# Nine more steps of a graph layer's running maximum get their rows by single-row DMAs from SyncE

## The chip, the cores and the metric

The kernel runs on one core of one Trainium2 chip. The core has TensorE (PE), VectorE (DVE), ScalarE (ACT), GpSimd (POOL) and SyncE (SP), which hands out DMAs; sixteen DMA engines move the data. The metric is the device time of one execution in microseconds; the time before is the median of three runs.

## The reference

```python
# x: [6250, 256]; src, dst: [100000] node numbers, sorted by dst
x_src, x_dst = x[src], x[dst]
theta_x = (x_dst - x_src) @ theta_w.T + theta_b
phi_x = x_src @ phi_w.T + phi_b
e = relu(theta_x + phi_x)
out = segment_max(e, dst, num_segments=x.shape[0])
out = where(isfinite(out), out, 0.0)
y = layernorm(x + out, axis=-1)          # no scale, no shift, eps 1e-5
```

## The kernel before

An edge's message is relu(A[dst] + B[src]) with A = x theta^T + both biases and B = x (phi - theta)^T. As A[dst] is the same for all edges of a node, the kernel takes the maximum of B[src] over the edges of each node and adds A afterwards.

**Tiling.** The 100,000 edges are split over the 128 partitions, 782 to each, in order. A step is one edge of every partition: 128 rows of B of 1 KB each. DVE folds the steps one after the other with one instruction (L720): the new running maximum is max(min(former, reset), row), where `reset` starts a new node. Three steps are a group (GROUP = 3, `START[g]` to `STOP[g]`); there are 261 groups, g = 0 to 260.

**Stages.** First TensorE makes the table B (L523), ACT copies it out of PSUM, SP writes it to HBM as `b_table` (L309); meanwhile POOL fetches 51 steps of rows of x (L385) into `early`. Then comes the main loop over the groups, from about 76 to 970 us. After it, POOL and DVE mend the nodes whose edges cross partitions (fix rows: L404, L413), POOL gathers the maxima by node (L422), and DVE and ACT add A and normalise (L836 to L855, L508), stored by SP (L370, L372).

**Where a step's rows come from.** `row_at(k)` (L694) names the place. 703 steps are gathered by POOL, one indirect DMA of 128 rows each, with the row numbers in `idx` (L397), into one of SLOTS = 18 places of `rows`; ahead of a group POOL waits until the fold that last used the place of the group's last row is done (L395). 51 steps, the first of groups 8, 10, 12 to 108, take x rows fetched early, which TensorE turns and multiplies and ACT copies back into `early` (L539, L547, L456, L460). 28 steps are products of TensorE with one-hot columns (L571, L753) and lie in `far`.

**Order on the engines.** Each engine's queue is written out by hand, and each runs `for g in range(NG)`:

- DVE: three folds, in the first 25 groups the splitting of the table for TensorE (L736, L744), one-hots (L753) and small work. The first two folds write PSUM (`acc`), the third writes `hist`. The third waits until the store of group g - 6 has landed (`s_hout`, HELD = 6), the first until ACT has copied group g - 2.
- ACT: in the first groups the casts of a table pair (L448, L452, which waits for the pair), then the copy of the group's two maxima from PSUM to `hist` (L468), after the folds of the group and the landing of the store of g - 6.
- SP: in groups 1 to 23 the load of table pair g + 1 (L328, into two buffers; it waits until DVE has made the rest of pair g - 1, `s_rest`), seven times a list of sources (L342), then the store of the group's maxima to HBM (L354), which waits for ACT's copy. Twelve times x rows follow (L357, L360), and from group 232 on tiles of x for A (L318).

Groups from LATE = 253 on are folded in `hist` alone.

Small tensors that the change touches: `none` (a row of -FLT_MAX, the former of the first fold, written to HBM at L311), `fix` (set to -FLT_MAX, later filled by L404), `bias2`, `ones` and `diag`, which are read in the preparation before the loop.

Of the kernel before, what the change touches and what calls it, by code (L numbers as in the profile page):

```python
# [5 lines left out]
P = 128  # L6
ALU = mybir.AluOpType
# [6 lines left out]
FLT_MAX = 3.4028234663852886e38  # L14
# [8 lines left out]
AT_ONCE = 4  # L23
HOT = 6
PRODUCT_SPANS = ((27, 61, 6), (61, 95, 6), (95, 123, 6), (123, 151, 6), (151, 179, 6), (179, 205, 6), (205, 231, 5))


def build(nc, x, xt, src, src_t, dst, theta_t, phi_t, theta_b, phi_b, out):
# [31 lines left out]
    for b, (begin, stop, apart) in enumerate(PRODUCT_SPANS):  # L60
        for t in range(NT):
            HOT_AT[begin + 4 + t * (stop - begin - 4) // NT].append((b, t))
        first = stop + 6 if stop % 2 else stop + 7
        BATCH_GROUPS.append([first + apart * j for j in range(AT_ONCE)])
        for j, g in enumerate(BATCH_GROUPS[b]):
            assert START[g] not in EARLY_OF and g < NG and (b + 1 == PRODUCTS or g < PRODUCT_SPANS[b + 1][1] + 2)
            PRODUCT_OF[START[g]] = (b, j)
    SPLIT_BY = PAIRS + 2
    EVACUATE_AT = {stop: b for b, (_, stop, _) in enumerate(PRODUCT_SPANS)}
# [22 lines left out]

    GATHERED = [k for k in range(STEPS) if k not in EARLY_OF and k not in PRODUCT_OF]
    PLACE = {k: i % SLOTS for i, k in enumerate(GATHERED)}
# [16 lines left out]
    with ExitStack() as ctx:  # L111
        def sb(name, shape, dt=F32):
            return ctx.enter_context(nc.sbuf_tensor(name, shape, dt))
# [23 lines left out]
        assert KC * AT_ONCE * P <= 4 * D  # L137
        far = sb("far", [P, AT_ONCE, D])
        sources = sb("sources", [P, AT_ONCE, P], I32)
        short_sources = sb("short_sources", [P, 2, AT_ONCE * P], I16)  # L140
        theta_sb = sb("theta_sb", [P, KC, D])
        diff_sb = sb("diff_sb", [P, KC, D])
        bias = sb("bias", [P, D])
        bias2 = sb("bias2", [P, D])

# [5 lines left out]
        reset = sb("reset", [P, STEPS])  # L151
        none = sb("none", [P, D])
        hi = sb("hi", [P, STEPS], BF16)
# [22 lines left out]
        ident = sb("ident", [P, P])  # L176
        ones = sb("ones", [P, P])
        small = sb("small", [P, 16])
        fix_row = sb("fix_row", [P, 1], I32)
        diag = sb("diag", [P, P])  # L180
        carry_on = sb("carry_on", [P, P])
        scanned = sb("scanned", [P, KC, P + 1])
        fix = sb("fix", [P, D])
        late_max = sb("late_max", [P, D])
        is_fix = sb("is_fix", [P, LATE_STEPS])
# [47 lines left out]
        s_got = [sem(f"rows_gathered{i}") for i in range(LANDED)]  # L233
        s_got_end = sem("last_row_gathered")
        s_fold = sem("steps_folded")
        s_copied = sem("groups_copied")
# [46 lines left out]
        def _(sp):  # L283
# [40 lines left out]
            def load_pair(i):  # L324
# [3 lines left out]
                sp.dma_start(b_pair[:, i % 2, 0:n], pairs[:, 2 * i:2 * i + n]).then_inc(s_pair[i % 2], 16)  # L328

            sp.wait_ge(s_bout[0], 16 * (CHUNKS + 1) // 2)  # L330
            sp.wait_ge(s_bout[1], 16 * (CHUNKS // 2))
            for i in range(2):
                load_pair(i)
            for g in range(NG):
                if 1 <= g < PAIRS - 1:
                    load_pair(g + 1)
                if g in SOURCES_AT:
                    b = SOURCES_AT[g]
                    if b:
                        sp.wait_ge(s_short, b)  # L340
                    k0, apart = START[BATCH_GROUPS[b][0]], START[BATCH_GROUPS[b][1]] - START[BATCH_GROUPS[b][0]]
                    sp.dma_start(sources[:], by_step[:, k0:k0 + (AT_ONCE - 1) * apart + 1:apart, :].broadcast_to(  # L342
                        [P, AT_ONCE, P])).then_inc(s_sources, 16)
                if g == A_FROM - 2:
                    sp.wait_ge(s_hotused, PRODUCTS * NT)
                    for t in range(2 * CHUNK):
                        load_tile(t)
                n, slot = STOP[g] - START[g], g % HELD * GROUP
                if g < LATE:
                    sp.wait_ge(s_copied, g + 1)  # L350
                else:
                    sp.wait_ge(s_fold, STOP[g])
                to = kept_by_p[:, START[g]:STOP[g], :] if g < LATE else late_by_p[:, START[g] - KEPT:STOP[g] - KEPT, :]
                sp.dma_start(to, hist[:, slot:slot + n, :]).then_inc(s_hout[g % HELD], 16)  # L354
                if g == EMPTIED:
                    sp.wait_ge(s_pad, 1)
                    sp.dma_start(x_sb[0:LAST_ROWS, NT - 1, :], x[(NT - 1) * P:N]).then_inc(s_x, 16)  # L357
                if g in X_AT:
                    i = X_AT[g]
                    sp.dma_start(x_sb[:, i * X_TILES:(i + 1) * X_TILES, :], by_load[i]).then_inc(s_x, 16)  # L360
                if g - 1 in A_AT:
                    for t in A_AT[g - 1]:
                        if t + 2 * CHUNK < NT:
                            load_tile(t + 2 * CHUNK)
# [13 lines left out]
        def _(pool):  # L378
# [12 lines left out]
            for g in range(NG):  # L391
# [4 lines left out]
                for k in these:  # L396
# [3 lines left out]
                    ).then_inc(s_got[g % LANDED] if k < STEPS - 1 else s_got_end, 16)  # L400

            for i in range(HELD):
                pool.wait_ge(s_hout[i], 16 * len(range(i, LATE, HELD)))
# [4 lines left out]
            pool.wait_ge(s_ends, 1)  # L408
            pool.wait_ge(s_noneout, 16)
            for i in range(HELD):  # L410
# [18 lines left out]
        def _(act):  # L429
            act.dma_start(dwin, dst).then_inc(s_dst, 16)  # L430
            act.dma_start(bias[:], theta_b.rearrange("(a d) -> a d", a=1).broadcast_to([P, D])).then_inc(s_bias, 16)
            act.dma_start(bias2[:], phi_b.rearrange("(a d) -> a d", a=1).broadcast_to([P, D])).then_inc(s_bias, 16)

# [79 lines left out]
        def _(pe):  # L513
# [14 lines left out]
            pe.wait_ge(s_const, 1)  # L528
            pe.matmul(ps_b[:, 0, 0:P], ones[:], diag[:], start=True, stop=True).then_inc(s_flags, 1)
            pe.wait_ge(s_const, 2)  # L530
# [82 lines left out]
        def _(dve):  # L613
# [26 lines left out]
            nc.vector.memset(edges[:, 0:1], 0.0)  # L640
            nc.vector.memset(ones[:], 1.0)
            nc.vector.memset(fix[:], -FLT_MAX)
            nc.vector.memset(late_max[:], -FLT_MAX)
# [40 lines left out]

            then(nc.vector.tensor_scalar(diag[:], ident[:], small[:, 1:2], None, ALU.mult))
            dve.wait_ge(s_bias, 32)
            nc.vector.tensor_tensor(bias[:], bias[:], bias2[:], ALU.add).then_inc(s_const, 1)
            dve.wait_ge(s_const, 1)
# [5 lines left out]
            def row_at(k):  # L694
                if k in PRODUCT_OF:
                    return far[:, PRODUCT_OF[k][1], :]
                return rows[:, PLACE[k], :] if k in PLACE else early[:, EARLY_OF[k], :]

            former = none[:]
            for g in range(NG):  # L700
                n, slot, at = STOP[g] - START[g], g % HELD * GROUP, g % 2 * 2
                if START[g] in EARLY_OF:
                    dve.wait_ge(s_cbe, EARLY_OF[START[g]] + 1)
                if START[g] in PRODUCT_OF:
                    dve.wait_ge(s_far, 2 * PRODUCT_OF[START[g]][0] + 2)
# [196 lines left out]
```

## Time and profile before

| | |
|---|---|
| median of 3 runs | 1057.68 us (1057.27 to 1057.81) |
| profiled execution: time / span | 1059.1 us / 1057.2 us |
| busy, share of the span | POOL 787.2 us (74%), PE 705.7 (67%), DVE 646.7 (61%), ACT 313.2 (30%) |
| DMA | 250.67 MB, mean 237 GB/s |
| granted TensorE clock, mean | 0.846 |

The span runs from the first to the last instruction of the profiled execution. "SPq" is SP's queue of DMA instructions: its times are those of handing out a DMA, not of moving the data, and the busy shares don't count them. For a DMA of POOL the busy time is that of making its descriptors. "issue" as the cause of idle time means that the engine waited for nothing that the profile shows. A wait is put down to whoever ended it last.

### The profile page before, as it was taken

Reading aid. Unit: us, or ns where it says so; the run is one execution under the profiler, and the core shown is the slowest. Engines: PE = TensorE matmul, PEld = TensorE weight load, DVE = VectorE, ACT = ScalarE, POOL = GpSimd, SP = SyncE. Lnnn points to the kernel's source line nnn. Section 1 sums busy time; section 2 is a strip of 40 time slices with the busy share of each in tenths; the row PEclk is TensorE's granted clock in tenths of the full one; section 3 lists DMA queues with packets and bytes.
Section 4 is the critical chain, followed back from the end, with each engine's and each line's share of the span. In section 5 each row is a group of like instructions: output and inputs, shape, how many; then the busy total and the mean of one; then the engine's idle time right before and its main releaser. Section 6 shows DMA issues by size and latency. Waiting matters only on the chain. (4 is left out here: it accounts for less than half of the span.)

```text
span 1057.2 us, 11054 instructions
## 1 busy us (share of the span) xinstructions
PE 705.7 (67%) x3014; PEld 374.4 (35%) x3067; DVE 646.7 (61%) x1585; ACT 313.2 (30%) x653; POOL 787.2 (74%) x812
## 2 busy tenths in 40 slices
PE   5923345999799979885887687668849866663000
PEld 4821223444455444432333233323313324442000
DVE  5006777665666657664655555555655555667898
ACT  2314565433433342223222221222121111110244
POOL 6777777777777777777777777777777777775773
PEclk9965555999899998998999699979979997986555
DMA  8967888777777777777777777777776678885465
GB/s 248 382 222 244 266 269 275 253 228 232 227 244 227 246 232 241 222 252 228 227 231 249 227 233 245 234 228 232 233 224 222 211 229 296 292 277 173 140 190 156
DMA packets 120631, 250.67 MB, mean 237 GB/s; under 512 B 19205, under 2 KB 61146, under 8 KB 120570
## 3 DMA queue, kind: packets, MB, share of 16 engines
q1 hardware_dynamic: 81498, 143.77, 38.0%
q0 software_dynamic: 38640, 105.53, 35.4%
q10 hardware_dynamic: 432, 0.66, 0.3%
q8 instruction: 24, 0.39, 0.2%
q14 instruction: 37, 0.30, 0.1%
HBM read 134.47 MB, written 115.45 MB: 236 GB/s over the span
## 5 line engine op out<-in xcount | busy, mean ns | idle before, releaser
L397 POOL DMA_INDIRECT rows<-b_table,idx x703 | 682.2, 970 | 214.2 <-issue 186.4
L571 PE MATMUL ps_a<-work,shared 128*128 128x512 bf16 x2008 | 475.2, 389 | 75.2 <-DVE work L753 71.7
L571 PEld LDWEIGHTS ps_a<-work,shared 128*128 128x128 bf16 x2058 | 198.1, 100 | 325.2 <-issue 63.0
L468 ACT COPY hist<-acc 128x512 f32<-128x512 f32 x253 | 148.2, 586 | 548.0 <-DVE hist L720 547.9
L720 DVE SCALAR_TENSOR_TENSOR acc<-hist,reset,rows 128x256 f32<-128x256 f32 x173 | 85.4, 494 | 251.8 <-issue 144.1
L720 DVE SCALAR_TENSOR_TENSOR acc<-acc,reset,rows 128x256 f32<-128x256 f32 x253 | 124.7, 493 | 31.0 <-DMA rows<-b_table,idx 19.1
L720 DVE SCALAR_TENSOR_TENSOR hist<-acc,reset,rows 128x256 f32<-128x256 f32 x253 | 122.3, 483 | 26.6 <-DVE acc L720 0.9
L547 PE MATMUL ps_b<-diff_sb,conv_t 128*128 128x256 f32 x204 | 69.8, 476 | 68.4 <-ACT conv_t L460 68.4
L753 DVE TENSOR_SCALAR work<-short_sources,node 128x512 bf16<-128x512 int16 x343 | 114.4, 373 | 0.3 <-PE ps_a L571 0.2
L595 PE MATMUL ps_a<-theta_sb,shared 128*128 128x256 f32 x196 | 57.0, 447 | 37.6 <-DVE shared L791 29.8
L547 PEld LDWEIGHTS ps_b<-diff_sb,conv_t 128*128 128x128 f32 x204 | 45.4, 234 | 83.1 <-ACT conv_t L460 73.9
L422 POOL DMA_INDIRECT rows<-runmax,end_row x49 | 52.1, 1063 | 16.3 <-issue 14.6
L556 PE MATMUL ps_d<-hi,row_of 128*128 128x270 bf16 (+1 forms) x95 | 35.0, 369 | 43.6 <-DVE row_of L762 43.3
L385 POOL DMA_INDIRECT early<-in_x,idx x51 | 49.5, 971 | 18.9 <-issue 15.2
L595 PEld LDWEIGHTS ps_a<-theta_sb,shared 128*128 128x128 f32 x196 | 41.9, 224 | 52.5 <-issue 46.0
L473 ACT ACTIVATE ps_d<-ps_d,node_up 128x782 f32<-128x782 f32 x49 | 43.9, 896 | 0.0
L557 PE MATMUL ps_d<-lo,row_of 128*128 128x512 bf16 x98 | 35.1, 377 | 3.3 <-DVE row_of L762 3.1
L508 ACT ACTIVATE hist<-hist,shift,rstd 128x256 f32<-128x256 f32 x49 | 25.7, 589 | 29.6 <-DVE shift L821 29.6
L556 PEld LDWEIGHTS ps_d<-hi,row_of 128*128 128x128 bf16 x98 | 10.2, 104 | 67.8 <-DVE row_of L762 59.2
L539 PE MATMUL ps_t<-ident,early 128*128 128x128 f32 x102 | 23.3, 317 | 13.1 <-DMA early<-in_x,idx 13.1
L452 ACT CAST shared<-work 128x512 bf16<-128x512 f32 (+1 forms) x25 | 15.2, 609 | 55.6 <-DMA work<-b_table 42.0
L539 PEld LDWEIGHTS ps_t<-ident,early 128*128 128x128 f32 x102 | 17.0, 168 | 23.9 <-issue 16.0
(133 smaller groups left out, 490.1 us busy)
## 6 DMA issues: line engine op xcount, KB each, us to landing
runmax<-hist SPq DMA_DIRECT2D x260, 384.0 KB, 3.1
rows<-b_table,idx POOLq DMA_INDIRECT x703, 3.5
b_table<-rows SPq DMA_DIRECT2D x7, 896.0 KB, 9.1
shared<-in_xt SPq DMA_DIRECT2D x49, 128.0 KB, 4.2
work<-b_table SPq DMA_DIRECT2D x24, 256.0 KB, 3.9
early<-in_x SPq DMA_DIRECT2D x12, 512.0 KB
out<-hist SPq DMA_DIRECT2D x11, 512.0 KB, 3.0
shared<-in_xt SPq DMA_DIRECT2D x7, 512.0 KB, 9.0
```

The source lines that it names most:

```text
L385: pool.indirect_dma_start(out=early[:, e, :], out_offset=None, in_=x, in_offset=bass.IndirectOffsetOnAxis(ap=idx[:, k:k + 1], axis=0)).the ...
L397: pool.indirect_dma_start(out=rows[:, PLACE[k], :], out_offset=None, in_=b_table, in_offset=bass.IndirectOffsetOnAxis(ap=idx[:, k:k + 1], ...
L422: pool.indirect_dma_start(out=rows[:, slot + i, :], out_offset=None, in_=runmax, in_offset=bass.IndirectOffsetOnAxis(ap=end_row[:, t + i:t ...
L468: nc.scalar.copy(hist[:, slot:slot + n - 1, :], acc[:, at:at + n - 1, :]).then_inc(s_copied, 1)
L473: nc.scalar.activation(dst_rows[:, 0:STEPS], dst_rows[:, 0:STEPS], ACT.Sign, bias=node_up[:, t:t + 1], scale=-1.0, accum_out=in_row[:, t:t ...
L539: mm = pe.transpose(ps_t[:, 0, k * P:(k + 1) * P], early[:, e, k * P:(k + 1) * P], ident[:])
L547: mm = pe.matmul(ps_b[:, 0, :], conv_t[:, k, :], diff_sb[:, k, :], start=(k == 0), stop=(k == KC - 1))
L556: pe.matmul(dst_rows[:, at:at + n], row_of[:], hi[:, at:at + n], start=True, stop=False)
L571: mm = pe.matmul(ps_a[k][:].rearrange("p j d -> p (j d)"), split[:, part, t, k * P:(k + 1) * P], hot[:, i % HOT, :], start=(t == 0 and par ...
L595: mm = pe.matmul(ps_a[t % 2][:, 0, :], xt_late[:, t % (2 * CHUNK), k, :], theta_sb[:, k, :], start=(k == 0), stop=(k == KC - 1))
L720: nc.vector.scalar_tensor_tensor(new, former, reset[:, k:k + 1], row_at(k), ALU.min, ALU.max).then_inc(s_fold, 1)
L753: nc.vector.tensor_scalar(hot[:, i % HOT, :], short_sources[:, b % 2, :], node[:, t:t + 1], None, ALU.is_equal).then_inc(s_hot, 1)
```

## The change

Nine steps, the first of nine odd groups (or the next free ones) after group 26, 52, ..., are taken from POOL's list. Their 1,152 rows are fetched by SP: behind the store of each of the groups 0 to 230 it hands out five DMAs (two at the last), each of one row of `b_table` to one partition of `direct`. The row's address comes from a register of SP; before every sixteenth row sixteen registers are loaded from the table of row numbers in HBM. `direct` holds three steps; from the fourth on, SP waits for the fold of three direct steps before. DVE waits for the 128 rows of a direct step before its group. To make room in SBUF, `none` shares `fix`, and `bias2`, `ones` and `diag` lie in `far`; POOL waits for the write of the empty row before it gathers the fix rows.

```diff
--- before.py
+++ after.py
@@ -22,6 +22,10 @@
+DIRECT = 9
+DIRECT_SLOTS = 3
+ROWS_A_GROUP = 5
+LOADED = 16
@@ -65,6 +69,14 @@
+    DIRECT_OF = {}
+    for m in range(DIRECT):
+        g = -(-P * (m + 1) // ROWS_A_GROUP) + 3
+        while START[g] in EARLY_OF or START[g] in PRODUCT_OF:
+            g += 1
+        DIRECT_OF[START[g]] = m
+    DIRECT_STEPS = list(DIRECT_OF)
+    assert len(DIRECT_STEPS) == DIRECT and DIRECT_STEPS[-1] < START[NG - 8] and P % LOADED == 0
@@ -90,7 +102,7 @@
-    GATHERED = [k for k in range(STEPS) if k not in EARLY_OF and k not in PRODUCT_OF]
+    GATHERED = [k for k in range(STEPS) if k not in EARLY_OF and k not in PRODUCT_OF and k not in DIRECT_OF]
@@ -136,12 +148,16 @@
+        direct = sb("direct", [P, DIRECT_SLOTS, D])
...
-        bias2 = sb("bias2", [P, D])
+        bias2 = far[:, 0, :]
+        ones = far[:, 1, 0:P]
+        diag = far[:, 1, P:2 * P]
...
+        none = fix
@@ -232,6 +246,7 @@
+        s_direct = [sem(f"rows_loaded_one_by_one{m}") for m in range(DIRECT)]
@@ -327,6 +342,20 @@
+            held = {}
+
+            def load_row(i):
+                m, p = divmod(i, P)
+                if p == 0 and m >= DIRECT_SLOTS:
+                    sp.wait_ge(s_fold, DIRECT_STEPS[m - DIRECT_SLOTS] + 1)
+                if p % LOADED == 0:
+                    k = DIRECT_STEPS[m]
+                    held["rows"] = nc.values_load_multi_w_load_instructions(
+                        src_t[k:k + 1, p:p + LOADED], engines=[mybir.EngineType.SP], min_val=0, max_val=N - 1,
+                        skip_runtime_bounds_check_because="src holds row numbers of x")[1]
+                sp.dma_start(direct[p:p + 1, m % DIRECT_SLOTS, :],
+                             b_table[bass.ds(held["rows"][p % LOADED], 1), :]).then_inc(s_direct[m], 16)
+
@@ -352,6 +381,8 @@
                 sp.dma_start(to, hist[:, slot:slot + n, :]).then_inc(s_hout[g % HELD], 16)
+                for i in range(ROWS_A_GROUP * g, min(ROWS_A_GROUP * (g + 1), DIRECT * P)):
+                    load_row(i)
                 if g == EMPTIED:
@@ -399,6 +430,7 @@
+            pool.wait_ge(s_noneout, 16)
             for i in range(HELD):
                 pool.wait_ge(s_hout[i], 16 * len(range(i, LATE, HELD)))
...
-            pool.wait_ge(s_noneout, 16)
@@ -638,8 +669,7 @@
-            nc.vector.memset(fix[:], -FLT_MAX)
@@ -694,6 +724,8 @@
+                if k in DIRECT_OF:
+                    return direct[:, DIRECT_OF[k] % DIRECT_SLOTS, :]
@@ -701,6 +733,8 @@
+                if START[g] in DIRECT_OF:
+                    dve.wait_ge(s_direct[DIRECT_OF[START[g]]], 16 * P)
```

## Rows read from the trace of the kernel before

**Rows 1.** Waits of POOL: who waited for whom, us in total, times, longest.
```profile
POOL rows L397 <- issue: 186.4, 612, 0.3
POOL rows L397 <- DVE hist L720: 14.3, 47, 0.3
POOL rows L397 <- DVE acc L720: 13.4, 44, 0.3
```

**Rows 2.** Line 397 (gathers): duration ns min/median/max, first and last start us.
```profile
L397 POOL DMA_INDIRECT rows<-b_table,idx x703: 942/946/1425, 70.6 to 965.7; - x176
```

**Rows 3.** The chain that ended last, around the last gather: start us, us, what.
```profile
961.77 1.12 POOL rows L397
962.89 0.30 issue
963.20 3.00 DMA rows<-b_table,idx
```

**Rows 4.** Waits of SP's queue, whole span.
```profile
SPq L354 <- ACT hist L468: 694.6, 245, 13.7
SPq L328 <- DVE work L744: 52.0, 23, 4.1
```

**Rows 5.** Line 397 by stretch: window us, length, busy us (x started), clock, DMA, GB/s.
```profile
70.00:110.00 40.00, 30.26 (x30) 0.50 0.67 208
110.00:170.00 60.00, 46.59 (x45) 0.53 0.89 277
```

**Rows 6.** Line 720 (folds) by the same stretches.
```profile
70.00:110.00 40.00, 13.21 (x27) 0.50 0.67 208
110.00:170.00 60.00, 22.66 (x47) 0.53 0.89 277
```

**Rows 7.** Waits in the stretch from 110 to 170 us, one row.
```profile
ACT shared L452 <- DMA work<-b_table: 28.5, 16, 3.3
```

**Rows 8.** Timeline of SP's queue, 110 to 170 us: start us, us, operation, count.
```profile
113.14 0.33 SPq L354 DMA_DIRECT2D runmax<-hist  x1
114.99 0.36 SPq L328 DMA_DIRECT2D work<-b_table  x1
...
166.53 0.33 SPq L354 DMA_DIRECT2D runmax<-hist  x1
169.27 0.33 SPq L328 DMA_DIRECT2D work<-b_table  x1
```

**Rows 9.** Timeline of SP's queue later (merged pieces last from first start to last end).
```profile
170.96 88.30 SPq L354 DMA_DIRECT2D runmax<-hist  x32
...
262.81 100.43 SPq L354 DMA_DIRECT2D runmax<-hist  x34
...
866.96 0.32 SPq L354 DMA_DIRECT2D runmax<-hist  x1
867.33 6.71 SPq L318 DMA_DIRECT2D shared<-in_xt  x14
```

**Rows 10.** Line 354 (store of maxima): duration ns min/median/max.
```profile
L354 SPq DMA_DIRECT2D runmax<-hist x261: 319/320/477, 78.2 to 970.4; - x131
```

**Rows 11.** Lines 370 (106 rows stored) and 311 (one row stored), the same.
```profile
L370 SPq DMA_DIRECT2D out<-hist x1: 264/264/264, 987.9 to 987.9; - x1
...
L311 SPq DMA_DIRECT2D runmax<-none x1: 471/471/471, 59.1 to 59.1; - x1
```

**Rows 12.** Line 372 (output stores of SP): time to landing.
```profile
DMA to landing us min/median/max: 1.7/3.0/3.2
```

**Rows 13.** DMA view: SP's queue (packets, MB, share), then two of its issues.
```profile
q1 hardware_dynamic: 81498, 143.77, 38.0%
...
runmax<-hist SPq DMA_DIRECT2D x260, 384.0 KB, 3.1
...
runmax<-none SPq DMA_DIRECT2D x1, 1.0 KB
```

**Rows 14.** All engines by stretch; last three numbers: clock, DMA share, GB/s.
```profile
260.00:430.00 170.00, 150.68 (x692) 80.68 (x705) 110.29 (x277) 62.70 (x140) 129.48 (x134) 0.94 0.73 236
```

More of the change, by code:

```diff
@@ L143, in build @@
         bias = sb("bias", [P, D])
-        bias2 = sb("bias2", [P, D])
+        bias2 = far[:, 0, :]
+        ones = far[:, 1, 0:P]
+        diag = far[:, 1, P:2 * P]
+        assert D == 2 * P
         early = sb("early", [P, max(EARLY, NT), D])
@@ L151, in build @@
         reset = sb("reset", [P, STEPS])
-        none = sb("none", [P, D])
         hi = sb("hi", [P, STEPS], BF16)
@@ L176, in build @@
         ident = sb("ident", [P, P])
-        ones = sb("ones", [P, P])
         small = sb("small", [P, 16])
         fix_row = sb("fix_row", [P, 1], I32)
-        diag = sb("diag", [P, P])
         carry_on = sb("carry_on", [P, P])
@@ L431, in _ @@
             act.dma_start(bias[:], theta_b.rearrange("(a d) -> a d", a=1).broadcast_to([P, D])).then_inc(s_bias, 16)
-            act.dma_start(bias2[:], phi_b.rearrange("(a d) -> a d", a=1).broadcast_to([P, D])).then_inc(s_bias, 16)
+            act.dma_start(bias2, phi_b.rearrange("(a d) -> a d", a=1).broadcast_to([P, D])).then_inc(s_bias, 16)
             for t in range(NT):
@@ L528, in _ @@
             pe.wait_ge(s_const, 1)
-            pe.matmul(ps_b[:, 0, 0:P], ones[:], diag[:], start=True, stop=True).then_inc(s_flags, 1)
+            pe.matmul(ps_b[:, 0, 0:P], ones, diag, start=True, stop=True).then_inc(s_flags, 1)
             pe.wait_ge(s_const, 2)
@@ L640, in _ @@
             nc.vector.memset(edges[:, 0:1], 0.0)
-            nc.vector.memset(ones[:], 1.0)
-            nc.vector.memset(fix[:], -FLT_MAX)
+            nc.vector.memset(ones, 1.0)
             nc.vector.memset(late_max[:], -FLT_MAX)
@@ L683, in _ @@
             nc.vector.tensor_copy(lo[:], pos.bitcast(I32))
-            then(nc.vector.tensor_scalar(diag[:], ident[:], small[:, 1:2], None, ALU.mult))
+            then(nc.vector.tensor_scalar(diag, ident[:], small[:, 1:2], None, ALU.mult))
             dve.wait_ge(s_bias, 32)
-            nc.vector.tensor_tensor(bias[:], bias[:], bias2[:], ALU.add).then_inc(s_const, 1)
+            nc.vector.tensor_tensor(bias[:], bias[:], bias2, ALU.add).then_inc(s_const, 1)
             dve.wait_ge(s_const, 1)
```

## The prediction

> **What bounds the kernel now.** I read the shares of the engines on the page first: no engine is full, POOL is the fullest, so the question is what its idle time is made of. The view of POOL's waits answers it: nearly all the idle time before the gathers of L397 is "issue", 0.30 us at a time, and the 91 idle times put down to DVE are no longer than 0.3 us each either [rows 1]. So POOL never waits; 0.30 us is the gap that each gather has. The view of line 397 gives 703 gathers between 70.6 and 965.7 us [rows 2], that is 895.1 / 702 = 1.275 us a gather (0.946 median duration, 0.30 gap, and some longer ones). The end of the chain shows that this is what sets the end: gathers back to back, the landing of the last, then the last steps [rows 3]. Behind the last fold some 87 us follow (fix rows, maxima by node, normalisation) that the change leaves alone. The bound is thus the number of gathers on POOL, as long as three others keep up: DVE's folds, ACT's copies, and SP, which stores each group's maxima and has so far mostly waited: 694.6 us for ACT's copies at L354, 52.0 us at L328 [rows 4].
>
> How much room is there? POOL may run 18 gathers ahead of the folds (SLOTS). Up to 170 us the windows count 30 + 45 = 75 gathers [rows 5] and 27 + 47 = 74 folds [rows 6]; nine of those folds (groups 8, 10 to 24) took a row of `early`, so 65 used a gather: POOL is 10 ahead. It needs the last row of a group free, so 18 - 10 - 3 = 5 gathers are left, 6.4 us. The reason for that lead is the loop of table pairs in the first 25 groups: SP loads a pair (L328) when DVE has freed the buffer, ACT waits for it (28.5 us in the stretch from 110 to 170 us) [rows 7], and ACT's copy of the group follows. This stretch runs at 3.8 us a group, slower than POOL; afterwards the folds catch up, 32 stores in 88.3 us (2.76 us each) and then 34 in 100.4 us (2.95 us) [rows 9].
>
> **The change part by part.**
>
> Nine gathers leave POOL: 9 x 1.275 = **11.5 us off**, all on the path, since POOL does not wait [rows 1, 2]. What is late next if POOL is faster is what the rest of this part is about.
>
> SP gets, in each of the groups 0 to 230, five DMAs of one row after the store, 1,152 in all, and before every sixteenth a load of sixteen registers from HBM, 72 in all. What a row costs on SP: a store of 128 rows takes 0.320 us when SP has waited [rows 10]; the one store of 106 rows takes 0.264 us, and the only one-row DMA of the trace 0.471 us, right behind another DMA [rows 11]. The fourteen DMAs at 867 us stand 6.71 / 14 = 0.48 us apart [rows 9]. So the ends are 0.26 + 0.03 (the gap between two issues) = 0.29 us and 0.47 + 0.04 = 0.51 us a row. I take 0.35: small DMAs seem cheaper than full ones, and the first behind the store pays the longer time; the register in the address adds something that no row shows. Five are **1.75 us** (1.45 to 2.55).
>
> The register load is not in the trace. Its lower end is another instruction that SP hands out without waiting, 0.3 us; its upper end, if the sixteen values come in one trip, is the round trip of a short transfer, 1.7 to 2.0 us with 1.7 the shortest landing on SP's queue [rows 12]. I take 1.7, since the load must wait for its data: 1.7 x 5/16 = **0.53 us** a group (0.1 to 0.6). If each value had a trip of its own, even at 0.32 us, it would be 5.1 us a load and 1.6 us a group. The Trainium skill ("Runtime: NRT & Kernel Launch", section "Instruction fetch mechanics") puts a bulk register load at about 200 ns a register, 3.2 us for sixteen; no row here shows it. By it the group would cost SP 0.47 us more, the pair loop would suffer most, and the time would come out near 1060 us, no gain.
>
> With the store and its gap (0.37 us) SP's work is then 0.37 + 1.75 + 0.53 = **2.65 us a group**. Its other DMAs in this stretch (23 pairs, 7 lists of sources, 11 loads of x) add some 18 us in all. SP can be at the store of group 231 no sooner than 78.2 + 18 + 231 x 2.65 = 708 us, against 867.0 us now [rows 9] and 855.5 us wanted. The break-even is (855.5 - 96) / 231 = 3.29 us a group over the whole, 2.76 to 2.95 in the quick groups 24 to 90, where six groups of `hist` and the 18 slots lend some time. At 2.65 this is hidden, with little to spare.
>
> Not hidden is the **pair loop**. What SP is moved past counts: behind the five rows and the register load the next L328 is queued, for it ACT waits, and behind ACT the copy of the group and DVE. From the start of a store to the next L328 there are 1.85 us at 113.1 and 2.74 us at 166.5 [rows 8]; the fifteen such gaps between have a mean of 2.2. With the change they are 0.37 + 1.75 = 2.1 us, and 3.8 us in a group with a register load, about one in three. The mean delay is 0.3 x 1.6 + 0.1 = 0.6 us for each pair; as the loop goes over two groups it costs 0.3 us a group, 5 us over groups 8 to 24, nothing before, where the gaps are 2.7 to 4.4 us. The landings of the pairs get longer by the extra packets; I allow 0.4 us for each of 8 turns, 3 us. Against these 8 us stand at best the 6.4 us of slots from above; but SP's rows also slow the catching-up after 170 us, so I count 3 of them: **5 us back** on POOL's path (0 with cheap rows, 12 with rows at 0.51 us and no cover).
>
> The other edits have one answer. `none` shares `fix`, `bias2`, `ones` and `diag` lie in `far`, one memset goes: all of it is before 76 us, where DVE waits, or has long been read when `far` (group 63) and `fix` (after the last steps) are written; if that cover were gone it would be one memset, under 0.5 us. POOL's wait for the empty row moves ahead of the fix gather; that row was written at 59 us. DVE waits for nine direct steps, each three or more groups (8 us) after its last row was issued, against a landing of 3.1 us for a store [rows 13]. SP's own wait for a slot of `direct` names a fold some 50 groups back. The bytes are the same as before.
>
> **The sum.** 1059.1 us is the profiled execution's own time (span 1057.2). 1059.1 - 11.5 + 5 + 0.5 (waits) = 1053.1 us. The median of the runs shown, 1057.68, lies 1.4 below the profiled one, so for timed runs I predict **1051.7 us**.
>
> **Rivals.**
>
> *SP becomes the bound* (slower). One mechanism: rows cost their upper end, 0.51 us, because every DMA keeps its issuer busy for about as long as the full ones at 867 us [rows 9, 11]. SP then needs 0.37 + 2.55 + 0.53 = 3.45 us a group, and reaches group 231 at 96 + 231 x 3.45 = 893 us, 26 us later than now: 1083.7 us. ACT's copies wait for the stores (`maxima_written`), DVE for both, POOL for the folds. It decides from 3.29 us a group, rows at 0.48 us; sixteen separate trips would do it as well, and by more. For it: the only one-row DMA took 0.471 us. Against it: that DMA had the last full chunk of the table before it, and the 106-row store was short.
>
> *The pair loop takes it all* (no change): rows at 0.40 us with the register load at 2.0 us or more, or no cover in the slots; 11.5 us go into 5 + 6 us of delay in the first 25 groups, 1057.7 us, give or take 2. For it: ACT already waits 28.5 us there [rows 7].
>
> *One DMA engine fills up* (slower). Of the packets on SP's queue, 81,498, the issues of the DMA view account for 81,496 if every DMA of 128 rows is its data packets and 16 more (a store 128 + 16, and so on for the 18 kinds listed from the store to the one-row write), which leaves two for the one-row write of 1 KB [rows 13]: one with data and one for the semaphore, so a row isn't spread over the engines. If all rows go to the same engine, it gets ten packets a group. Its share is 0.73 now [rows 14]; the mean packet of that queue takes 0.38 x 16 x 1057.2 / 81,498 = 0.079 us, which makes 0.79 us of 3.0 and a share of 0.99 in the quick groups, 0.95 later. At 0.104 us a packet it would need 0.73 x 3.0 + 1.04 = 3.23 us a group there, 0.23 too much for 85 groups: +20 - 11.5 = 8 us slower, 1066 us. It decides from 0.081 us a packet. Against it: the share counts waiting too, and the load of one engine moves landings, not POOL's pace, while slots are left. The Trainium skill ("DMA: Bandwidth & Descriptors", section "Why a DMA increments its semaphore by 16 and not by 1") says that a DMA of SP uses the lowest-numbered engines, so all 1,152 rows would be on the first; the trace agrees with the two packets, not with the place, which it doesn't show.
>
> *The change doesn't do what it says*: a direct row lands after the fold that wants it, so that DVE waits nine times. Even 5 us each would be hidden in part, since POOL runs ahead: no change, 1057.7 us.
>
> **How the numbers follow.** The forecast, faster by over 2.1 us, has 0.54: the middle values give it, and only the costs of SP are unknown. The pair loop cancelling it 0.13, direct rows late 0.02; SP as bound 0.23, the packed engine 0.08. So faster 0.54, same 0.15, slower 0.31; 0.2% (2.1 us) is about what a measurement of this kernel can tell from no change. The forecast's own range is 1046.2 (all 11.5 us, nothing back) to 1055.5 us. For 8 times in 10 the range must take in the cancelled case, the packed engine and SP as bound up to the upper end of the bounds, 1084 us; what is left out is dearer register loads and a gain above 11.5.
>
> **What would show it.** Right: 694 gathers at the same 1.27 us, the last one some 6 us earlier; row DMAs of 0.3 to 0.4 us on SP; SP's waits for ACT shrinking to about 100 to 200 us but still there in groups 112 to 230; ACT's waits for pairs up by 5 to 10 us; POOL with a few real waits for DVE around 150 to 200 us. Wrong: SP without waits at L354, POOL waiting for DVE all along, ACT's copies waiting for SP's stores, which means rows above 0.48 us; or gathers that take far longer to land than the 3.0 us of the last one now [rows 3], which means the packed engine; or no waits of POOL at all, the full 11.5 us.

## The result

| | median | beside the kernel before |
|---|---|---|
| before | 1057.74 us (1057.27 to 1058.06, 4 runs) | |
| after | 1120.92 us (1118.43 to 1123.06, 4 runs) | ratio 1.060, 95% interval 1.058 to 1.061 |

The change makes the kernel 63 us slower, 6%; the forecast was 6 us faster, and the time lies above the range. The profiled execution has a span of 1121.2 us (1057.2 before), a mean granted clock of 0.814 and 224 GB/s.

The costliest groups of the page of the changed kernel (out<-in, count, busy us and mean ns, idle time before and what ended most of it):

```profile
L428 POOL DMA_INDIRECT rows<-b_table,idx x694 | 671.1, 967 | 289.9 <-issue 181.5
...
L754 DVE SCALAR_TENSOR_TENSOR hist<-acc,reset,rows 128x256 f32<-128x256 f32 x253 | 122.4, 484 | 260.9 <-DMA runmax<-hist 247.5
...
L754 DVE SCALAR_TENSOR_TENSOR acc<-hist,reset,direct 128x256 f32<-128x256 f32 x9 | 4.5, 496 | 62.9 <-DMA direct<-b_table 62.9
```

A gather costs the same as before (967 ns in the mean, 970 before), but DVE now stands 247.5 us before the third fold of a group, the one that may write `hist` only when the store of six groups before has landed. The waits of POOL and of SP's queue say the same from both ends; in [rows 1] POOL's idle time put down to DVE was 27.7 us, all of it gaps of 0.3 us, and in [rows 4] SP waited 694.6 us for ACT. Now there are (waiting engine, for whom, us in total, times, longest):

```profile
POOL rows L428 <- DVE acc L754: 76.6, 75, 9.1
...
POOL rows L428 <- DVE hist L754: 31.8, 45, 5.5
```

```profile
SPq L383 <- ACT hist L499: 53.9, 37, 16.0
```

The chain of waits is closed: SP is late with the store, DVE waits for its landing, POOL for the fold. Between 80 and 949 us SP's waits for ACT at the store are only 14.5 us in all, and from 180 us on there are next to none:

```profile
SPq L383 <- ACT hist L499: 3.5, 8, 1.2
```

SP is full. The timeline of its queue shows with what (start us, us, operation, count; a merged piece lasts from its first start to its last end):

```profile
308.25 0.35 SPq L383 DMA_DIRECT2D runmax<-hist  x1
308.78 1.87 SPq L356 DMA_DIRECT2D direct<-b_table  x5
310.69 0.35 SPq L383 DMA_DIRECT2D runmax<-hist  x1
311.23 5.34 SPq L356 DMA_DIRECT2D direct<-b_table  x5
316.62 0.36 SPq L383 DMA_DIRECT2D runmax<-hist  x1
```

A group without a register load takes 2.4 to 2.5 us, one with a load 5.9 us. The views of lines 353 (register loads) and 356 (rows) give the parts (duration ns min/median/max):

```profile
L353 SPq TENSOR_LOAD <-in_src_t_ptr x72: 1012/1157/2000, 78.0 to 937.9; - x72
L353 SPq ALU_OP  x72: 42/44/53, 79.1 to 939.5; - x72
L353 SPq TENSOR_LOAD <-in_src_t x72: 1711/1906/2284, 79.2 to 939.5; - x72
```

```profile
L356 SPq FUSED_REGOPS  x1152: 37/37/51, 81.2 to 948.8; - x192
L356 SPq MOVE direct<-b_table x1152: 29/29/29, 81.3 to 948.9; - x192
L356 SPq DMA_DIRECT2D direct<-b_table x1152: 224/228/1127, 81.3 to 949.0; - x192
```

One call that loads sixteen values is three instructions: a load of the table's address, 1.16 us, a sum, and the load of the values, 1.91 us; with the gaps 3.3 us. A row is 0.228 + 0.037 + 0.029 us and gaps; five of them last 1.87 to 1.97 us in the timeline, 0.39 us a row. So a group costs SP 0.355 (store) + 0.18 (up to the first row) + 5 x 0.39 + 3.3 x 5/16 + 0.04 = **3.56 us**, where 3.29 us was the break-even of the prediction. The last store before the tiles of x for A, that of group 231, shows the sum of it; before it stood at 866.96 us [rows 9]:

```profile
949.25 0.36 SPq L383 DMA_DIRECT2D runmax<-hist  x1
949.66 7.00 SPq L333 DMA_DIRECT2D shared<-in_xt  x14
```

That is 82 us late, and yet the end is only 64 us late. The rest is given back afterwards: when SP let go, POOL had its slots full of gathers in advance, and the last 29 groups ran faster than POOL. The last gather started at 965.7 us before [rows 2] and starts at 1029.9 us now.

### The profile page after: what moved, and what is told of

Read it like the earlier page. It is cut to its first block and busy times, and to the rows that moved or that the text cites. A ratio compares the mean times of both kernels' runs of the same rounds, so it can differ in the third digit from the quotient of the medians.

```text
span 1121.2 us, 14780 instructions
## 1 busy us (share of the span) xinstructions
PE 719.0 (64%) x3067; PEld 377.9 (34%) x3067; DVE 636.5 (57%) x1584; ACT 313.4 (28%) x653; POOL 776.0 (69%) x803
## 3 DMA queue, kind: packets, MB, share of 16 engines
q1 hardware_dynamic: 83802, 144.96, 36.0%
## 5 line engine op out<-in xcount | busy, mean ns | idle before, releaser
L428 POOL DMA_INDIRECT rows<-b_table,idx x694 | 671.1, 967 | 289.9 <-issue 181.5
L602 PE MATMUL ps_a<-work,shared 128*128 128x512 bf16 x2058 | 491.4, 396 | 98.5 <-DVE work L787 98.1
L602 PEld LDWEIGHTS ps_a<-work,shared 128*128 128x128 bf16 x2058 | 202.6, 101 | 358.0 <-issue 87.4
L754 DVE SCALAR_TENSOR_TENSOR hist<-acc,reset,rows 128x256 f32<-128x256 f32 x253 | 122.4, 484 | 260.9 <-DMA runmax<-hist 247.5
L754 DVE SCALAR_TENSOR_TENSOR acc<-hist,reset,rows 128x256 f32<-128x256 f32 x164 | 79.7, 486 | 17.3 <-DMA rows<-b_table,idx 6.1
L626 PE MATMUL ps_a<-theta_sb,shared 128*128 128x256 f32 x196 | 54.1, 426 | 33.5 <-DVE shared L825 18.8
L587 PE MATMUL ps_d<-hi,row_of 128*128 128x512 bf16 x98 | 37.7, 385 | 50.2 <-DVE row_of L796 50.0
L626 PEld LDWEIGHTS ps_a<-theta_sb,shared 128*128 128x128 f32 x196 | 39.2, 210 | 48.4 <-issue 27.1
L754 DVE SCALAR_TENSOR_TENSOR acc<-hist,reset,direct 128x256 f32<-128x256 f32 x9 | 4.5, 496 | 62.9 <-DMA direct<-b_table 62.9
L770 DVE TENSOR_TENSOR shared<-work,shared 128x512 bf16<-128x512 f32 (+1 forms) x25 | 17.0, 681 | 35.4 <-ACT shared L479 35.4
```

What stands on the lines that cost most here:

```text
L428: pool.indirect_dma_start(out=rows[:, PLACE[k], :], out_offset=None, in_=b_table, in_offset=bass.IndirectOffsetOnAxis(ap=idx[:, k:k + 1], ...
L587: pe.matmul(dst_rows[:, at:at + n], row_of[:], hi[:, at:at + n], start=True, stop=False)
L602: mm = pe.matmul(ps_a[k][:].rearrange("p j d -> p (j d)"), split[:, part, t, k * P:(k + 1) * P], hot[:, i % HOT, :], start=(t == 0 and par ...
L626: mm = pe.matmul(ps_a[t % 2][:, 0, :], xt_late[:, t % (2 * CHUNK), k, :], theta_sb[:, k, :], start=(k == 0), stop=(k == KC - 1))
L754: nc.vector.scalar_tensor_tensor(new, former, reset[:, k:k + 1], row_at(k), ALU.min, ALU.max).then_inc(s_fold, 1)
```

## The experiments

Theory A: SP's own time is the bound. Theory B: the packets of the one-row DMAs fill one DMA engine. Theory C: the delay of the table pairs in the first 25 groups makes most of the loss. The comparisons fell into two conditions: in some the kernel before took 1058 us, as in the result, in others it took 1292 to 1305 us, on other chips. The kernel before has no trace there; the changed kernels' traces have idle gaps that the first ones don't, as in the waits of POOL's gathers that are put down to nothing ("issue"; f1, then e1, the same kernel on the other side):

```profile
POOL rows L423 <- issue: 176.7, 580, 0.3
...
POOL rows L423 <- issue: 190.9, 608, 1.7
```

Ratios are to the kernel before in the same comparison, and can differ by some tenths of a per cent from the quotient of the two medians; the two conditions stand apart.

**The change again** (f0). No edit.

> The changed kernel as it is, once more, beside the kernel before: in the last comparison the kernel before itself took 1292 us, with idle gaps of all engines that the first traces don't have, so those four runs are compared again from here on. Expected: 1118 to 1123 us beside 1057.7 if this run is like the first; if the kernel before takes about 1290 us again, the change is slower there by about as much as the numbers-in-SBUF run was (1.11) or more.

Two runs, 1125.0 us and 1560.4 us, beside 1058.2 us. The first and its trace repeat the result (span 1123.2 us); no other run comes near the second, it isn't explained, and there is no ratio.

**Fixed addresses** (f1, e1).

```diff
-                if p % LOADED == 0:
-                    k = DIRECT_STEPS[m]
-                    held["rows"] = nc.values_load_multi_w_load_instructions(...)[1]
-                sp.dma_start(direct[p:p + 1, m % DIRECT_SLOTS, :],
-                             b_table[bass.ds(held["rows"][p % LOADED], 1), :]).then_inc(s_direct[m], 16)
+                sp.dma_start(direct[p:p + 1, m % DIRECT_SLOTS, :],
+                             b_table[p:p + 1, :]).then_inc(s_direct[m], 16)
```

> All 1,152 one-row DMAs with fixed addresses (row p for partition p, so the direct steps get other rows than they should), no register loads. Theory A, SP's own time is the bound: SP needs 0.35 + 0.04 + 5 x 0.31 = 1.9 us a group (a row of fixed address took 0.264 us in the disturbed run) and waits again for ACT; 1046 to 1050 us. Theory B, the packets of the rows fill one DMA engine: all still there, about 1120 us.

1048.13 us beside 1058.22, ratio 0.991 (0.989 to 0.993). The span is 1045.7 us, 11.5 less than before. SP waits again, and a row takes 0.268 us:

```profile
SPq L378 <- ACT hist L494: 335.7, 206, 13.6
```

```profile
L351 SPq DMA_DIRECT2D direct<-b_table x1152: 214/268/1009, 78.0 to 854.6; - x192
```

All 1,152 one-row DMAs and their packets are in this kernel, so theory B falls. Of the 9 x 1.275 us for the nine gathers the span has all and the medians have 10.1 us. What the loss hangs on are the register loads and the register work of the rows.

Under the other condition the same kernel took 1309.7 us beside 1292.6, ratio 1.012 (1.008 to 1.017):

> The changed kernel with all its 1,152 one-row DMAs, but with fixed addresses (row p of the table for partition p, so the nine direct steps get other rows than they should) and without the 72 register loads. Theory A, SP's own time is the bound (3.5 to 3.8 us a group): without the loads (1.05 us a group) and the register work (0.12 us a row) SP needs about 0.5 + 5 x 0.27 = 1.9 us a group and goes back to waiting; about 1048 us, all 11.5 us gained less 1 or 2 in the first 25 groups. Theory B, the packets of the one-row DMAs fill one DMA engine: they are all still there, so the time stays near 1120 us.

**Row numbers in SBUF** (f2, e4). SP brings the 128 numbers of a direct step to SBUF a step ahead and loads its registers from there; `direct` has two slots in place of three.

```diff
+        numbers = sb("numbers", [1, 2, P], I32)
...
+            def load_numbers(m):
+                sp.dma_start(numbers[0:1, m % 2, :],
+                             src_t[DIRECT_STEPS[m]:DIRECT_STEPS[m] + 1, :]).then_inc(s_numbers[m % 2], 16)
...
-                        src_t[k:k + 1, p:p + LOADED], engines=...
+                        numbers[0:1, m % 2, p:p + LOADED], engines=...
```

> Row numbers brought to SBUF by nine DMAs, sixteen registers loaded from there; two slots of direct rows; right output. The register load took 1.24 us there in the disturbed run, against 3.3 us for the pair from HBM. Theory A: SP needs 0.55 + 5 x 0.39 + 0.4 = 2.9 us a group, below the 2.95 to 3.6 us of most groups: 1049 to 1056 us. Theory B: unchanged, 1120 us.

1050.02 us beside 1058.22, ratio 0.992 (0.990 to 0.994): the change's idea at work, 8 us faster than before and about 71 us faster than the change in the result. The address load is gone, the value load a little shorter:

```profile
L364 SPq TENSOR_LOAD <-numbers x72: 1149/1623/2172, 81.5 to 845.8; - x72
```

SP needs 0.355 + 0.18 + 1.95 + 1.7 x 5/16 + 0.04 = 3.06 us a group. It is just enough: between 170 and 440 us SP waits 3.4 us in all for ACT.

```profile
SPq L394 <- ACT hist L510: 3.4, 7, 0.9
```

Under the other condition this kernel is 10.7% slower than the kernel before, 1427.6 us beside 1292.6 (1.098 to 1.115):

> The changed kernel with the row numbers of a direct step brought to SBUF by one DMA of 512 bytes ahead of it, and the sixteen registers loaded from there (to make room two slots of direct rows in place of three); right output. The pair of loads from HBM (1.16 us for the pointer, 1.91 us for the values) becomes one. Theory A: if it takes about 1.1 us, SP needs 0.5 + 5 x 0.39 + 0.35 = 2.8 us a group, about the pace of the quick groups: 1050 to 1056 us; if it takes 1.9 us as from HBM, 3.05 us a group and 1058 to 1068 us. Theory B (packets): unchanged, 1120 us.

There the rows and their register work have the same medians (the value load 1.24 us, even less than the 1.62 us above), but single ones last over a microsecond (maximum of the register work 1.38 us, against 0.051 us in the change) and idle gaps come between them. From start to start two rows stand 0.78 us apart in the mean in e4's trace, 0.44 us in f2's. SP has no room for that:

```profile
L367 SPq FUSED_REGOPS  x1152: 1/37/1380, 112.5 to 1217.5; - x192
...
L367 SPq DMA_DIRECT2D direct<-b_table x1152: 2/228/1402, 112.6 to 1217.7; - x192
```

**Three rows a group** (f3, e3). `DIRECT = 5`, `ROWS_A_GROUP = 3`.

> Three rows a group and five direct steps, loads from HBM; right output. Theory A: SP needs 0.55 + 3 x 0.39 + 3/16 x 3.3 = 2.35 us a group; 6.4 us gained less 3 to 6 us of the pair loop, 1052 to 1056 us. Theory B: 6 packets a group, about 1051 us. Theory C, the pair loop costs more than the gain: above 1058 us.

1053.56 us beside 1058.22, ratio 0.995 (0.994 to 0.997): 4.7 of 6.4 us arrive. SP at 0.575 + 3 x 0.39 + 3.3 x 3/16 = 2.36 us a group waits 302.5 us for ACT. Under the other condition 1320.2 us (three runs) beside 1292.6, ratio 1.020 (1.014 to 1.026):

> The changed kernel with three rows a group and five direct steps (in place of five rows and nine steps); right output. Theory A: SP needs 0.5 + 3 x 0.39 + 3/16 x 3.3 = 2.3 us a group, under the 2.75 to 2.95 us of the quick groups; 5 x 1.275 = 6.4 us gained less 3 to 6 us of the pair loop, 1052 to 1056 us. Theory B: 6 packets a group in place of 10, share of the engine about 0.9, 1051 us. Theory C: the pair loop alone costs more than 6 us, above 1058 us.

**Four rows a group** (i1, g1). `DIRECT = 7`, `ROWS_A_GROUP = 4`.

> Four rows a group, seven direct steps, SP at 2.94 us a group. Where the kernel before takes 1058 us: 1051 to 1056 us by theory A, 1060 us or more if the break-even lies below 2.9 us a group; beside 1305 us again 1.086.

1054.78 us beside 1057.95, ratio 0.997 (0.996 to 0.999): 3.2 of 8.9 us arrive, with SP at 0.575 + 4 x 0.39 + 3.3 x 4/16 = 2.96 us a group. Under the other condition 1417.9 us beside 1305.1, ratio 1.087, and in a repeat 1.086 (1.080 to 1.092):

> Four rows a group, seven direct steps, loads from HBM; right output. One size changed, to place the break-even. Theory A: SP needs 0.55 + 4 x 0.39 + 4/16 x 3.3 = 2.94 us a group; over 224 groups with its other DMAs about 78 + 18 + 659 = 755 us, but in groups 24 to 90, where 2.75 to 2.95 us are wanted, it just keeps up. 7 x 1.275 = 8.9 us gained less 4 to 7 us of the pair loop: 1051 to 1056 us. If the break-even lay lower than 2.9 us, 1060 us or more.

**Rows only from group 25 on** (i2, g2). `DIRECT = 8`, the direct steps lie 25 groups later (not shown), and in the loop:

```diff
-                for i in range(ROWS_A_GROUP * g, min(ROWS_A_GROUP * (g + 1), DIRECT * P)):
+                for i in range(max(0, ROWS_A_GROUP * (g - ROWS_FROM)),
+                               min(ROWS_A_GROUP * (g + 1 - ROWS_FROM), DIRECT * P)):
                     load_row(i)
```

> Five rows a group only from group 25 on, eight direct steps. Twice so far beside a kernel before of 1305 us (1.120 of it both times). Where the kernel before takes 1058 us: theory A (SP's pace) 1098 to 1110 us, theory C (pair loop) 1047 to 1055 us; beside 1305 us again 1.12.

1112.24 us beside 1057.95, ratio 1.052 (1.048 to 1.056). The pair loop is as quick as before, the last pair is handed out at 169.65 us (169.27 in [rows 8]), and the loss is nearly all there: 54 us with eight steps, against 63 us with nine. Theory C falls: SP's pace in the groups after the pair loop makes most of the loss. (The first row below is the last pair; from 180 us on SP waits for ACT 2.3 us in all.)

```profile
169.65 0.34 SPq L344 DMA_DIRECT2D work<-b_table  x1
171.67 4.85 SPq L384 DMA_DIRECT2D runmax<-hist  x3
179.97 2.00 SPq L357 DMA_DIRECT2D direct<-b_table  x5
182.02 0.36 SPq L384 DMA_DIRECT2D runmax<-hist  x1
```

Under the other condition 1463.8 us beside 1305.1, ratio 1.120 (1.116 to 1.124), in a repeat 1.120 again:

> Five rows a group as in the change, but only from group 25 on, so eight direct steps; loads from HBM; right output. It takes the rows and loads out of the groups with table pairs. Theory A, SP's pace is the bound: from group 25 (about 171 us) on 205 groups at 3.5 to 3.7 us, at group 231 about 171 + 205 x 3.6 + 8 = 917 us against 867 us before: 1098 to 1110 us. Theory C, the pair loop made most of the 63 us: 1047 to 1055 us.

**Thirty-two registers to a load** (i3, g3). `LOADED = 32`.

> The change with 32 registers to a load. The value load took 3.48 us for 32 registers against 1.9 us for 16, so about 0.1 us a register, and the pointer 1.1 us once a load: 4.6 us for 32 in place of 6.6 us, 0.3 us a group less. Where the kernel before takes 1058 us: SP at 3.3 us a group, 1078 to 1100 us; beside 1305 us again 1.14.

1079.58 us beside 1057.95, ratio 1.021 (1.019 to 1.023), 41 us faster than the change in the result. It halves the address loads, but a value load goes by the register:

```profile
L353 SPq TENSOR_LOAD <-in_src_t_ptr x36: 1022/1278/1862, 78.3 to 875.6; - x36
...
L353 SPq TENSOR_LOAD <-in_src_t x36: 3415/3782/4207, 79.5 to 876.7; - x36
```

3.78 us for 32 against 1.91 us for 16. SP needs 0.575 + 1.95 + 5.2 x 5/32 = 3.34 us a group. Under the other condition 1489.2 us beside 1305.1, ratio 1.140 (1.135 to 1.145), where the value load had a median of 3.48 us:

> The change with 32 registers to a load from HBM in place of 16 (36 loads); right output. It tells what a load's time goes by. If by the trip: the pair stays at 3.3 us, 0.52 us a group less, SP at 3.0 to 3.2 us a group and the time 1055 to 1075 us. If the value load goes by the register (1.9 us for 16, 3.8 us for 32): pair 5 us, 0.26 us a group less, about 60 us less work over 230 groups at most: 1075 to 1095 us.

**Numbers in SBUF, 32 to a load** (g4) ran only where the kernel before took 1305 us: 1437.7 us, ratio 1.101 (1.098 to 1.105).

> Row numbers in SBUF and 32 registers to a load; right output. Against the kernel with 16 to a load (1050.0 us, 1.62 us a load, where SP waited for ACT only 3.4 us between 170 and 440 us): if the load goes by the trip, 0.25 us a group less for SP and the time 1047 to 1050 us; if by the register, the same time, 1049 to 1051 us.

From SBUF too the load grows with the registers, 2.13 us for 32 there against 1.24 us for 16 in e4, though it doesn't double; whether it would gain beside 1058 us is open.

**Loads without rows** (h5, e2). The register loads stay, and fifteen of sixteen rows come with one DMA of fixed address; DVE waits for as many DMAs as there are (that line of the edit is not shown).

```diff
-                sp.dma_start(direct[p:p + 1, m % DIRECT_SLOTS, :],
-                             b_table[bass.ds(held["rows"][p % LOADED], 1), :]).then_inc(s_direct[m], 16)
+                if p % LOADED == 0:
+                    sp.dma_start(direct[p:p + 1, m % DIRECT_SLOTS, :],
+                                 b_table[bass.ds(held["rows"][0], 1), :]).then_inc(s_direct[m], 16)
+                    sp.dma_start(direct[p + 1:p + LOADED, m % DIRECT_SLOTS, :],
+                                 b_table[p + 1:p + LOADED, :]).then_inc(s_direct[m], 16)
```

> The 72 register loads at their places; of each 16 rows only the first has its address from a register, the other 15 come with one DMA of fixed address (other rows than they should be). Theory A: SP needs about 0.4 + 3.3 x 5/16 + 0.25 = 1.7 us a group and waits again; the loads delay only some table pairs. Fixed addresses gave 1048.1 us, so 1048 to 1052 us. Theory C, the loads among the table pairs cost most: above 1060 us.

It met the other condition both times: 1301.2 us beside 1305.4, ratio 0.997 (0.994 to 1.000), and before that 1284.8 beside 1292.6, ratio 0.996 (0.992 to 1.000). There, the 72 loads by themselves cost less than the nine gathers give (11.5 us would be 0.9%, and 0.3 to 0.4% arrive); only together with the rows do they fill SP. That speaks against theory C too. Beside 1058 us this kernel was not run.

> The changed kernel with the 72 register loads at their places, but of each 16 rows only the first has its address from a register; the other 15 come with one DMA of fixed address (other rows than they should be). So 144 DMAs in place of 1,152. Theory A: SP needs about 0.5 + 3.3 x 5/16 + little = 1.8 us a group; not the bound any more, about 1049 us, plus some us if the 3.3 us loads delay the table pairs of the first 25 groups. Theory B (packets): 1047 us. Theory C, the pair loop pays for most: the loads in groups 0 to 24 are untouched, and with them up to half of the loss, 1070 us or more.

**The runs in one table**, by SP's time for a group, worked out as above from the medians beside 1058 us (for f1 read from its timeline):

| kernel | direct steps | SP, us a group | time, us | gain by gathers alone | ratio beside 1292 to 1305 us |
|---|---|---|---|---|---|
| f1, fixed addresses | 9 | 2.1 | 1048.1 | 11.5 | 1.012 |
| f3, three rows | 5 | 2.36 | 1053.6 | 6.4 | 1.020 |
| i1, four rows | 7 | 2.96 | 1054.8 | 8.9 | 1.087 |
| f2, numbers in SBUF | 9 | 3.06 | 1050.0 | 11.5 | 1.107 |
| i3, loads of 32 | 9 | 3.34 | 1079.6 | 11.5 | 1.140 |
| i2, from group 25 | 8 | 3.56 | 1112.2 | 10.2 | 1.120 |
| the change | 9 | 3.56 | 1120.9 | 11.5 | not run |

The edge lies between 3.06 us a group, 8 us faster, and 3.34 us, 22 us slower. Beyond it every 0.1 us counts 231 times, up to 23 us: the 0.22 us between i3 and the change are 41 us. Where the kernel before takes 1300 us, the kernel of 2.1 us a group is 1.2% slower already, and those near 3 us or above lose 9 to 14%; their SP times are longer there than the column says.

## Why the prediction was wrong

**The bound and the gain were right.** POOL's gathers set the end, and with SP out of the way nine fewer give a span 11.5 us shorter (f1; 10.1 us in the medians), against the 9 x 1.275 of the sum.

**The step that failed is the price of the register load.** It was put at 1.7 us, with 2.0 us as the upper end "if the sixteen values come in one trip"; it took 3.3 us. Two things were missed. The table's address is loaded too, once for each load (1.16 us), and the values come one after the other, about 0.12 us each (1.91 us for 16, 3.78 us for 32). The prediction did write down the case of one trip for each value and priced it at 5.1 us, but named it only in passing under "SP becomes the bound", left dearer register loads out of its range, and let the bound end at 2.0 us: a bound drawn from the landing of another kind of DMA is no bound for an operation the trace doesn't have. The sum from the Trainium skill ("Runtime: NRT & Kernel Launch", section "Instruction fetch mechanics"), about 200 ns a register and 3.2 us for sixteen, agrees with the 3.3 us in total, though the trace divides it otherwise: over a third of it is the address, and the values alone take 0.12 us a register. It would have given no gain, "near 1060", still far from 1121, since the next term was off as well.

**The row was nearly right, and the two errors add.** 0.35 us was taken, 0.39 us measured (1.95 us in place of 1.75 a group), and the 0.18 us from the store to the first row was missing. 1.75 + 0.53 + 0.37 = 2.65 us became 1.95 + 1.03 + 0.58 = 3.56 us; the load is 0.50 us of the 0.91 us. By this sum neither alone crosses 3.29 us: with the load's true price it is 3.15 us (which no run has), with the true rows and pause 3.06 us. With 2.65 us this was "hidden, with little to spare"; the prediction's own formula gives 96 + 231 x 3.56 = 918 us for the store of group 231, and it stood at 949.25 us. Of the 31 us between, SP's waits are 16.6 us. The rest is that 3.56 us is a sum of medians: from the first store at 77.6 us to that of group 231 pass 871.6 us, and without the waits and the 18 us of its other DMAs this is 3.62 us a group, for single instructions take longer (up to 1.13 us for a row, 2.0 us for an address).

**The break-even was about right.** 3.29 us a group was predicted, the pace at which the whole gain still arrives; the runs have 3.06 us faster and 3.34 us slower, and none between. But past it the loss was undersized: by the formula, without waits and with medians, 3.34 us would put the store of group 231 at 867 us, no later than before; it came at 896.8 us in i3, and the kernel was 22 us slower. "Hidden" had no margin: 0.28 us a group lie between 8 us won and 22 lost.

**The pair loop was undersized, but it is not the cause.** 8 us of delay were counted, 5 of them on the path. The last pair is handed out at 189.12 us in the changed kernel, 20 us later than the 169.27 us of [rows 8]:

```profile
189.12 0.37 SPq L343 DMA_DIRECT2D work<-b_table  x1
189.54 0.42 SPq L383 DMA_DIRECT2D runmax<-hist  x1
```

Much of it is hidden by POOL's lead: up to 180 us POOL waited 11.0 us for DVE. With i2, which has none of it, the kernel is still 54 us slower than before; the change is 9 us slower than that and has one gather more taken off, 1.3 us, so the pair loop is worth some 10 us. In i1, where SP keeps its pace, 5.7 of 8.9 us are lost, and POOL's only long waits are 5.2 us at 168 us and 4.2 us at 185 us, about the last pair (183.5 us there); the loss is about the 5 us of the sum.

**The rivals.** "SP becomes the bound" is what happened, and it had 0.23. Its price, 1083.7 us, came from rows at 0.51 us and 3.45 us a group; the rows were cheap, and the loads, thought cheap, made it 3.56 us and 1120.9 us. "One DMA engine fills up" is refuted by f1. Its premise was right: SP's queue has 83,802 packets, 2,304 more than in [rows 13], two for each row,

```profile
q1 hardware_dynamic: 83802, 144.96, 36.0%
```

but their load doesn't show: gathers land after 3.4 us in the median. Whether all rows go to the same engine, as they would by the Trainium skill ("DMA: Bandwidth & Descriptors", section "Why a DMA increments its semaphore by 16 and not by 1"), is shown by no run. "The direct rows come late" is there as well, 62.9 us of DVE's waits in seven places, as much as the loss. It is a consequence of SP's lag, not its cause: SP, whose stores set the pace, waits for ACT only 3.5 us after 180 us, so DVE's waits can't have held it up; and in f2, with 22.9 us in three places, POOL never waits more than 2.5 us.

## What to carry to other kernels

A queue that waits 695 us isn't free for 695 us of work, since what counts is its work for each turn of the loop against the pace of that loop, and every excess is multiplied by the turns: write down the sum for a turn, and give every instruction that the trace has never shown a bound wide enough to cross the edge. A call that looks like one instruction may be three; loading values from a table in HBM paid for the address each time, and moving the 128 numbers to SBUF first took away half of it and turned 6% slower into 0.8% faster. A gain that leaves no room on a queue holds only where nothing disturbs it: the same kernel lost 10.7% where the kernel before itself took 1292 us.

## What the runs showed of the hardware

- A one-row DMA costs SP 0.214 to 0.228 us at least, against 0.32 us for a store of 128 rows [rows 10]. One behind the other, rows of fixed address (median 0.268 us) stand 0.32 us apart in f1, and rows with the address from a register (median 0.228 us and 0.066 us of register work) 0.41 us in the changed kernel, where full DMAs stand 0.48 us apart [rows 9].
- A register load: about 0.12 us for each register (1.91 us for 16, 3.78 for 32 from HBM; 1.62 us for 16 from SBUF, all beside 1058 us), and 1.16 us more where the tensor's address must be loaded.
- In the three comparisons on other chips the kernel before took 22 to 23% longer. The changed kernels' traces there have the same medians for gathers (0.946 us) and rows, idle gaps between POOL's gathers of up to 1.7 us that nothing in the profile explains (0.3 us in f1), and single register instructions of SP's rows of up to 1.38 us (0.051 us in the change). The cause was not looked for, and no run tells the chip from the time.
